# Where the rows of q and k stand: row 16 d + t instead of row 8 t + d

## The chip, the cores and the metric

The kernel runs on one core of one Trainium2 chip. Its time is the device time of one execution in microseconds (us). TensorE (PE in the profile) multiplies matrices, VectorE (DVE), ScalarE (ACT) and GpSimd (POOL) do the rest, and SyncE (SP) issues most of the transfers (DMAs). On-chip memory (SBUF) has 128 rows, called partitions.

## The reference, cut to what matters

The input x is 8 sequences of 256 tokens with 128 features. Three layers are added to it in turn:

```python
x = x + 0.5 * ffn(layernorm(x))      # router over 8 experts, top 2, hidden size 352
x = x + attention(layernorm(x))      # 16 heads of 8 dimensions
x = x + 0.5 * ffn(layernorm(x))
# in the attention, for each sequence b and head h:
q = q * cos + rotate_half(q) * sin;  k = k * cos + rotate_half(k) * sin
attn = q @ k.T * 8 ** -0.5 + alibi   # alibi: slope of the head * min(key - query, 0) * 8
w = softmax(attn);  out = w @ v
```

The change concerns only the product of q and k.

## The kernel before, in words

**Three phases.** `blocks(0)` is the first FFN: tokens are scattered by expert into 39 blocks of 128 rows, each block goes through the expert's matrices, and the results are scattered back. Then comes the attention with the second router, sequence by sequence. `blocks(1)` is the second FFN, built as the first one. The order of all instructions on every engine is written out by hand, and semaphores join the engines.

**q and k as sums of three bf16 parts.** After the rotation, q and k of one sequence are fp32. POOL and ACT cut them into three bf16 tiles that add up to the fp32 value: `lev[:, level, s, :]`, with level 0 (high), 1 and 2 (low), and s 0 for q and 1 for k (`split_qk`, lines 428 to 432, and `part`, line 649). In `lev` dimension d of head h stands in partition 16 d + h. The product q·k is formed from six products of parts, `PAIRS` = (0,0), (1,0), (2,0), (0,1), (1,1), (0,2) (level of q, level of k). They are added up by one matrix product over the partitions: in the tiles `qs` (q) and `ks` (k), pair t has eight rows, one for each dimension d, and each row holds all 16 heads × 256 tokens (8 KB).

**`stack(b)`** (lines 334 to 345) brings the parts of sequence b there: for each level, for q and k, one DMA on SP's queue for each pair that takes that level. These are 12 DMAs for a sequence, each of 64 KB: 128 runs of 512 bytes (one d and one h), read from 128 partitions of `lev` and written to 8 partitions of `qs` or `ks`, sixteen runs in each. The counts for a sequence are six DMAs of level 0, four of level 1 and two of level 2.

**The other rows.** Six rows of the same tiles carry the part of alibi that lies beyond 128 tokens (`far_in`, `far_rows`), the last two carry the negated row maximum of the scores (`max_rows`, lines 347 to 352, two DMAs of 8 KB), and the remaining rows are zero. There are three buffers (`RING`).

**Scores, twice.** `scores_1` (line 1139, 126 rows) makes the scores with queries on the partitions, so that DVE can find each query's maximum (`row_max`, line 923). `max_T` turns the maxima, ACT and DVE split them in two (lines 655 and 928), and `max_rows` puts them into the tile of q. `scores_2` (line 1160, 128 rows) then makes the scores with keys on the partitions, less the maximum, and ACT takes the exponential (line 662).

**Order.** In front of the loop, `stack(0)`, `stack(1)` and `max_rows(0)` stand on SP; PE does `scores_1` of sequence 0 and ACT the split of sequence 1 (line 649), which waits for all of `stack(0)`, since it overwrites `lev`. In iteration b of the loop each engine goes through steps 0 to 15: PE does `scores_2` of sequence b and `scores_1` of b + 1, and SP issues, in this order, `grow` (256 KB that `combine` needs), `stack(b + 2)` and `max_rows(b + 1)`. The first `scores_2` of the next iteration waits for `max_rows`. All these DMAs share one queue, so what stands in front of `max_rows` in it is served first.

Of the kernel before, what the change touches and what calls it, by code (L numbers as in the profile page):

```python
# [15 lines left out]
P = 128  # L16
TB = N // P
NT = B * TB
H, HD = 16, 8
# [21 lines left out]
YP_ROWS = SCRAP + P * ZR  # L41

PAIRS = [(0, 0), (1, 0), (2, 0), (0, 1), (1, 1), (0, 2)]
QK_ROWS = len(PAIRS) * HD

S2_ROWS = 128
S1_ROWS = S2_ROWS - 2
VW = 32
RING = 3
# [11 lines left out]
def macaron(nc, x, small_w, w1, v1, w2, ffn_bias, proj_b, slopes, ident, dist, dist_t, rope, expert_ids,  # L61
            far, ones_rows, out):
    ctx = ExitStack()
    with ctx:
        ctx.enter_context(nc.allow_low_precision(reason="exact splits"))

        def sb(name, shape, dt=F32):
            return ctx.enter_context(nc.sbuf_tensor(name, shape, dt))

        def sem(name):  # L70
            return ctx.enter_context(nc.semaphore(name))
# [22 lines left out]
        qs, ks = [qk_rows[:, i] for i in range(RING)], [qk_rows[:, RING + i] for i in range(RING)]  # L94
# [8 lines left out]
        lev = sb("lev", [P, 3, 2, N], BF16)  # L103
# [74 lines left out]
        d_far = nc.dram_tensor("d_far", (3, 2, H, N), BF16, kind="Internal").ap()  # L178
# [16 lines left out]
        far_out, rows_landed, bias_added, half_done = sem("far_out"), sem("rows_landed"), sem("bias_added"), sem("half_done")  # L195
# [54 lines left out]
        def _(sp):  # L250
# [23 lines left out]
            def blocks(r):  # L274
# [19 lines left out]
                for n in range(first, first + NB):  # L294
                    if n % GS == 0 and n + XB < first + NB:
                        rows += loaded(mybir.EngineType.SP, tab_r, (n + XB - first) // GS, BLOCK_ROWS - 1)
                    if n + XB < first + NB:
                        sp.wait_ge(xbT_full, n // GS + 1)
                        sp.wait_ge(dest_done, n // GS + 1)
                        load(n + XB)  # L300
                    if n == 6:
                        far_in()
                    if n == 30:
                        far_rows()
# [12 lines left out]
            def far_in():  # L317
                sp.wait_ge(wu_lo_done, 1)
                sp.dma_start(far_v, far).then_inc(far_landed, 16)
                sp.wait_ge(zero_done, 2 * RING)  # L320
                for i in range(RING):
                    sp.dma_start(qs[i][QK_ROWS:QK_ROWS + 3, :, :], ones_rows[0:3]).then_inc(rows_landed, 16)
                    sp.dma_start(ks[i][QK_ROWS + 3:QK_ROWS + 6, :, :], ones_rows[3:6]).then_inc(rows_landed, 16)
                    sp.dma_start(ks[i][S1_ROWS:S2_ROWS, :, :], ones_rows[6:8]).then_inc(rows_landed, 16)

            def far_rows():
                sp.wait_ge(far_step, 5)
                sp.dma_start(d_far.rearrange("l s h n -> h l s n"), far_l).then_inc(far_out, 16)
                sp.wait_ge(far_out, 16)
                for i in range(RING):  # L330
                    sp.dma_start(ks[i][QK_ROWS:QK_ROWS + 3, :, :], d_far[:, 0]).then_inc(rows_landed, 16)
                    sp.dma_start(qs[i][QK_ROWS + 3:QK_ROWS + 6, :, :], d_far[:, 1]).then_inc(rows_landed, 16)

            def stack(b):

                q, k = qs[b % RING], ks[b % RING]
                if b >= RING:
                    sp.wait_ge(s2_full, 16 * (b - RING + 1))
                for level, made in ((0, 2), (1, 4), (2, 5)):
                    sp.wait_ge(split_step, b * 5 + made)  # L340
                    for s, dst in ((0, q), (1, k)):
                        for t, pair in enumerate(PAIRS):
                            if pair[s] == level:
                                sp.dma_start(dst[t * HD:(t + 1) * HD, :, :], lev[:, level, s, :]  # L344
                                             ).then_inc(stack_landed[b % RING], 16)

            def max_rows(b):
# [3 lines left out]
                sp.wait_ge(ml_done, b + 1)  # L351
                sp.dma_start(q[S1_ROWS + 1:S2_ROWS, :, :], ml[:, 1, :]).then_inc(mrow_landed, 16)

            blocks(0)
            stack(0)
            stack(1)
            max_rows(0)
            for b in range(B):
                if b + 3 < B:
                    if b:  # L360
                        sp.wait_ge(comb[0], 4 * (b + 3))
                    sp.dma_start(grow, pairs(0, b + 3)).then_inc(g_landed, 16)
                if b + 2 < B:
                    stack(b + 2)
                if b + 1 < B:
                    max_rows(b + 1)
# [656 lines left out]
        def _(pe):  # L1023
# [127 lines left out]
            def scores_2(b, j):  # L1151
# [6 lines left out]
                for a in range(2):  # L1158
                    h = 2 * hp + a
                    nc.tensor.matmul(o[:, a * N:(a + 1) * N], ks[b % RING][0:S2_ROWS, h, kt * P:(kt + 1) * P],  # L1160
                                     qs[b % RING][0:S2_ROWS, h, :], start=(a == 0), stop=False)
                o = o[:, :].rearrange("p (h n) -> p h n", h=2)[:, :, kt * P:(kt + 1) * P]
# [155 lines left out]
```

## Time and profile before

| | us |
|---|---|
| median of 3 runs (lowest, highest) | 573.76 (571.87, 573.95) |
| profiled execution, its own time | 576.06 |
| its span, first to last instruction | 573.9 |
| PE busy | 399.3 |
| DVE busy | 301.4 |
| POOL busy | 250.3 |
| ACT busy | 214.5 |

The first FFN takes the span up to about 168 us, the attention up to about 442 us, and the rest is the second FFN. "Busy" counts the time in which an engine executes. The "granted clock" is the share of its full speed that TensorE was allowed in a stretch; it is 1.00 or 0.50. "DMA share" is the mean busy share of the core's 16 DMA engines in a stretch, GB/s what they moved. In a timeline, `[3.48 <-DMA ...]` at the end of a line says how long the engine was idle before it and what released it.

### The profile page before, as it was taken

What the parts mean: (1) busy time and instruction counts of PE and PEld (TensorE: products, weight loads), DVE (VectorE), ACT (ScalarE), POOL (GpSimd) and SP (SyncE); (2) the same over time, 40 slices, a digit from 0 to 9 for tenths busy, and PEclk for the clock granted to TensorE, in tenths of its full rate; (3) what the DMA queues carried; (4) which work ended last, traced back from release to release, by engine and by line L of the source; (5) the groups of instructions that cost most, each with busy time, mean ns of one, the idle gap of its engine ahead of it and who ended that gap; (6) DMA issues with size and microseconds to landing.
All of it is one profiled execution on the core that took longest, in us unless ns stands there. A gap on an engine that the chain in (4) does not pass through costs nothing.

```text
span 573.9 us, 9982 instructions
## 1 busy us (share of the span) xinstructions
PE 399.3 (70%) x3132; PEld 338.4 (59%) x3132; DVE 301.4 (53%) x909; ACT 214.5 (37%) x481; POOL 250.3 (44%) x358
## 2 busy tenths in 40 slices
PE   2500097999942378888878879798977119999970
PEld 2500087999941256575756657576754119999970
DVE  3960055598634175546465746465622406565545
ACT  5500043455411123535454444535465113444420
POOL 8677437388534310303434342423242422855440
PEclk9999999899985587989898989899999558999995
DMA  9921212122220550504133241413000021222217
GB/s 292 197 85 51 83 47 71 53 61 57 62 83 3 52 55 21 69 8 51 43 42 53 33 62 23 45 25 48 15 21 6 24 92 39 63 65 67 57 37 220
DMA packets 51030, 35.60 MB, mean 62 GB/s; under 512 B 5898, under 2 KB 48106, under 8 KB 50938
## 3 DMA queue, kind: packets, MB, share of 16 engines
q1 hardware_dynamic: 45940, 24.16, 22.7%
q0 software_dynamic: 4896, 10.54, 5.4%
q8 instruction: 27, 0.44, 0.4%
q10 hardware_dynamic: 144, 0.27, 0.2%
q14 instruction: 23, 0.19, 0.1%
HBM read 15.97 MB, written 12.55 MB: 50 GB/s over the span
## 4 chain that ended last, share of the span: by engine, by line
POOL 27%; PE 25%; issue 22%; DVE 10%; DMA 9%; ACT 4%; SPq 3%; POOLq 0%; DVEq 0%; ACTq 0%
POOL yp L408 12%; POOL xs L394 7%; PE bank L1139 5%; DMA qk_rows<-wd 5%; PE bank L1160 3%; PE bank L1175 3%; DVE nm L923 3%; PE bank L1142 2%; PE bank L1143 2%; DVE scr L915 2%; PE bank L1121 2%; POOL xres L458 1%; SPq L344 1%; PE bank L1163 1%; POOL rstd L383 1%
## 5 line engine op out<-in xcount | busy, mean ns | idle before, releaser
L923 DVE TENSOR_REDUCE nm<-bank 128x2 f32<-128x512 f32 x128 | 84.4, 686 | 68.6 <-PE bank L1143 67.4
L408 POOL DMA_INDIRECT yp<-scr,dest x78 | 76.4, 979 | 75.5 <-ACT scr L609 70.3
L662 ACT ACTIVATE stage<-bank 128x512 f32<-128x512 f32 x128 | 75.1, 596 | 85.0 <-PE bank L1164 83.9
L1063 PE MATMUL bank<-wu,xbT_hi 128*128 x156 | 65.7, 421 | 2.5 <-DVE xbT_lo L852 2.5
L1139 PE MATMUL bank<-qk_rows 126*128 126x256 bf16 x256 | 55.1, 300 | 17.0 <-DVE nm L923 9.6
L1078 PE MATMUL bank<-wd,scr 128*128 (+1 forms) x468 | 66.2, 278 | 0.3
L1078 PEld LDWEIGHTS bank<-wd,scr 128*128 128x128 f32 (+1 forms) x468 | 62.2, 194 | 0.6 <-issue 0.6
L1160 PE MATMUL bank<-qk_rows 128*128 128x256 bf16 x256 | 51.7, 285 | 11.6 <-DMA qk_rows<-wd 11.6
L859 DVE COPY scr<-bank 128x256 f32<-128x256 f32 x78 | 33.0, 424 | 49.7 <-PE bank L1072 49.3
L1054 PE MATMUL bank<-idn,scr 128*128 128x128 f32 x78 | 14.4, 297 | 62.7 <-DMA scr<-xs 62.7
L1065 PE MATMUL bank<-wu,xbT_hi 128*128 x156 | 52.5, 336 | 0.0
L1064 PE MATMUL bank<-wu,xbT_lo 128*128 x156 | 52.3, 335 | 0.0
L1142 PE MATMUL bank<-near_hi,idn_r 128*128 128x256 f32 x128 | 50.3, 393 | 0.0
L1054 PEld LDWEIGHTS bank<-idn,scr 128*128 128x128 f32 x78 | 10.7, 154 | 63.9 <-issue 63.3
L1163 PE MATMUL bank<-near_hi,idn_r 128*128 128x256 f32 x128 | 48.2, 377 | 0.0
L609 ACT ACTIVATE scr<-bank 128x128 f32<-128x128 f32 x78 | 21.7, 278 | 64.1 <-PE bank L1078 60.2
L873 DVE TENSOR_TENSOR scr<-bank,scr 128x352 f32<-128x352 f32 x78 | 40.8, 523 | 7.1 <-PE bank L1065 5.1
L428 POOL TENSOR_TENSOR scr<-scr 128x512 f32<-128x512 f32 x8 | 10.2, 1279 | 78.0 <-DVE scr L915 78.0
L852 DVE TENSOR_TENSOR xbT_lo<-bank,xbT_hi 128x384 fp32r<-128x384 f32 x26 | 14.4, 556 | 52.0 <-ACT xbT_hi L603 51.9
L619 ACT ACTIVATE scr<-bank 128x352 f32<-128x352 f32 x78 | 36.2, 464 | 13.2 <-PE bank L1065 13.2
L1072 PE MATMUL bank<-idn,scr 128*128 128x128 f32 (+1 forms) x234 | 39.7, 279 | 0.3 <-DVE scr L873 0.3
L603 ACT ACTIVATE xbT_hi<-bank 128x384 fp32r<-128x384 f32 x26 | 12.8, 490 | 70.6 <-PE bank L1054 70.6
(157 smaller groups left out, 901.8 us busy)
## 6 DMA issues: line engine op xcount, KB each, us to landing
qk_rows<-lev SPq DMA_DIRECT2D x96, 64.0 KB
scr<-xs SPq DMA_DIRECT2D x78, 64.5 KB
stage<-yp SPq DMA_DIRECT2D x11, 256.0 KB, 4.8
stage<-in_w SPq DMA_DIRECT2D x8, 176.0 KB, 3.9
stage<-in_v SPq DMA_DIRECT2D x8, 176.0 KB, 4.9
scr<-yp SPq DMA_DIRECT2D x5, 256.0 KB, 4.5
yp<-scr,dest POOLq DMA_INDIRECT x78
xres<-in_x SPq DMA_DIRECT2D x4, 256.0 KB, 5.0
```

The costliest lines, as they stand in the source:

```text
L408: nc.gpsimd.indirect_dma_start(out=yp[r][:, :], out_offset=bass.IndirectOffsetOnAxis(ap=dest[:, n:n + 1], axis=0), in_=ysb[:, n % YS, :], ...
L662: nc.scalar.activation(probs[:, g % RING, kt, 2 * (hp % 2):2 * (hp % 2) + 2, :], psS2[(b * 16 + j) % 3][:, :].rearrange("p (h n) -> p h n" ...
L873: nc.vector.tensor_tensor(hid[:, n % 2, :], up_v[n % 2][:, 0:F], gel[:, n % 2, :], ALU.mult).then_inc(hid_done, 1)
L923: nc.vector.tensor_reduce(nm[:, qt, 2 * hp:2 * hp + 2], psS1[i % 2][:, :].rearrange("p (h n) -> p h n", h=2), AX.X, ALU.max, negate=True). ...
L1063: nc.tensor.matmul(dst, hi, moving(n, a), start=True, stop=False)
L1064: nc.tensor.matmul(dst, lo, moving(n, a), start=False, stop=False)
L1065: nc.tensor.matmul(dst, hi, moving(n, a + 2 * F), start=False, stop=True).then_inc(done, 1)
L1078: i = nc.tensor.matmul(psH[n % 3][:, 3 * P:4 * P], hTs[0:w, n % 2, k * P:(k + 1) * P], wd[0:w, bass.ds(experts[n - first], 1), k, :].rearr ...
L1139: nc.tensor.matmul(o[:, j * N:(j + 1) * N], qs[b % RING][0:S1_ROWS, h, qt * P:(qt + 1) * P], ks[b % RING][0:S1_ROWS, h, :], start=(j == 0) ...
L1142: nc.tensor.matmul(o, idn_r[:, :], near_hi[0][:, 2 * hp:2 * hp + 2, :], start=False, stop=False)
L1160: nc.tensor.matmul(o[:, a * N:(a + 1) * N], ks[b % RING][0:S2_ROWS, h, kt * P:(kt + 1) * P], qs[b % RING][0:S2_ROWS, h, :], start=(a == 0) ...
L1163: nc.tensor.matmul(o, idn_r[:, :], near_hi[1][:, 2 * hp:2 * hp + 2, :], start=False, stop=False)
```

## The change

The eight rows of a pair no longer stand side by side. Dimension d of pair t goes to partition 16 d + t instead of 8 t + d, so each of the 12 DMAs writes to 8 partitions that stand 16 apart. The six alibi rows move from partitions 48 to 53 to 6 to 11, which pairs 0 to 5 leave free. Sizes and counts of all DMAs, and all operand shapes of TensorE, stay as they are.

```diff
 PAIRS = [(0, 0), (1, 0), (2, 0), (0, 1), (1, 1), (0, 2)]
-QK_ROWS = len(PAIRS) * HD
-S2_ROWS = 128
+SPREAD = P // HD
+FAR = len(PAIRS)
+S2_ROWS = P
@@ far_in
-                    sp.dma_start(qs[i][QK_ROWS:QK_ROWS + 3, :, :], ones_rows[0:3]).then_inc(rows_landed, 16)
-                    sp.dma_start(ks[i][QK_ROWS + 3:QK_ROWS + 6, :, :], ones_rows[3:6]).then_inc(rows_landed, 16)
+                    sp.dma_start(qs[i][FAR:FAR + 3, :, :], ones_rows[0:3]).then_inc(rows_landed, 16)
+                    sp.dma_start(ks[i][FAR + 3:FAR + 6, :, :], ones_rows[3:6]).then_inc(rows_landed, 16)
@@ far_rows
-                    sp.dma_start(ks[i][QK_ROWS:QK_ROWS + 3, :, :], d_far[:, 0]).then_inc(rows_landed, 16)
-                    sp.dma_start(qs[i][QK_ROWS + 3:QK_ROWS + 6, :, :], d_far[:, 1]).then_inc(rows_landed, 16)
+                    sp.dma_start(ks[i][FAR:FAR + 3, :, :], d_far[:, 0]).then_inc(rows_landed, 16)
+                    sp.dma_start(qs[i][FAR + 3:FAR + 6, :, :], d_far[:, 1]).then_inc(rows_landed, 16)
@@ stack
-                                sp.dma_start(dst[t * HD:(t + 1) * HD, :, :], lev[:, level, s, :]
+                                sp.dma_start(dst[t::SPREAD, :, :], lev[:, level, s, :]
                                              ).then_inc(stack_landed[b % RING], 16)
```

## Rows read from the trace of the kernel before

**Rows 1.** The page's chain that ended last, shares of the span by line.
```profile
POOL yp L408 12%; POOL xs L394 7%; PE bank L1139 5%; DMA qk_rows<-wd 5%; PE bank L1160 3%; PE bank L1175 3%; DVE nm L923 3%; PE bank L1142 2%; PE bank L1143 2%; DVE scr L915 2%; PE bank L1121 2%; POOL xres L458 1%; SPq L344 1%; PE bank L1163 1%; POOL rstd L383 1%
```
**Rows 2.** That chain in order of time: start us, duration us, what.
```profile
214.40 1.84 DMA qk_rows<-wd
...
240.60 5.07 DMA qk_rows<-wd
...
271.68 4.42 DMA qk_rows<-wd
...
364.01 4.83 DMA qk_rows<-wd
```
**Rows 3.** Timeline of PE at the first `scores_2` of sequences 1 to 6.
```profile
245.71 0.61 PE L1160 MATMUL bank<-qk_rows 128*128 128x256 bf16 x2 [3.48 <-DMA qk_rows<-wd]
...
276.14 0.55 PE L1160 MATMUL bank<-qk_rows 128*128 128x256 bf16 x2 [0.91 <-DMA qk_rows<-wd]
...
307.06 0.61 PE L1160 MATMUL bank<-qk_rows 128*128 128x256 bf16 x2 [1.36 <-DMA qk_rows<-wd]
...
338.09 0.61 PE L1160 MATMUL bank<-qk_rows 128*128 128x256 bf16 x2 [1.48 <-DMA qk_rows<-wd]
...
368.89 0.61 PE L1160 MATMUL bank<-qk_rows 128*128 128x256 bf16 x2 [1.40 <-DMA qk_rows<-wd]
...
398.05 0.38 PE L1160 MATMUL bank<-qk_rows 128*128 128x256 bf16 x2
```
**Rows 4.** Timeline of SP's queue: start us, us of issuing, line, transfers.
```profile
191.49 1.27 SPq L344 DMA_DIRECT2D qk_rows<-lev  x2
...
231.19 8.75 SPq L344 DMA_DIRECT2D qk_rows<-lev  x12
...
383.75 8.38 SPq L344 DMA_DIRECT2D qk_rows<-lev  x12
...
394.78 0.58 SPq L352 DMA_DIRECT2D qk_rows<-wd  x1
```
**Rows 5.** Stretches: window us, its length, granted clock, DMA share, GB/s.
```profile
186.00:187.00 1.00, 0.50 0.31 79
...
190.00:191.00 1.00, 0.50 0.65 61
...
198.00:199.00 1.00, 0.50 0.02 1
...
216.00:217.00 1.00, 0.50 0.42 123
...
393.00:394.00 1.00, 1.00 0.62 97
...
396.00:397.00 1.00, 1.00 0.04 9
```
**Rows 6.** Timeline in front of the loop: start us, us, engine, line.
```profile
184.74 23.56 SPq L344 DMA_DIRECT2D qk_rows<-lev  x24
...
193.18 1.41 DVE L915 TENSOR_TENSOR scr<-bank,rope_sb 64x512 f32<-64x512 f32 x2
194.73 1.26 POOL L428 TENSOR_TENSOR scr<-scr 128x512 f32<-128x512 f32 x1 [4.53 <-DVE scr L915]
...
199.82 0.63 ACT L649 ACTIVATE lev<-scr 128x512 bf16<-128x512 f32 x1 [9.52 <-DMA qk_rows<-lev]
199.82 0.58 PE L1139 MATMUL bank<-qk_rows 126*128 126x256 bf16 x2 [7.40 <-issue]
```
**Rows 7.** Stretches: window us, its length, PE busy, granted clock, DMA share, GB/s.
```profile
245.52:248.93 3.41, 3.22 (x15) 0.50 0.00 0
...
368.40:371.81 3.41, 2.92 (x14) 0.50 0.07 24
...
395.70:399.10 3.40, 3.02 (x33) 1.00 0.02 4
```
**Rows 8.** Waits: engine, line, waited for: us in total, times, longest us.
```profile
PE bank L1187 <- ACT scr L669: 14.3, 10, 1.8
```

## The prediction

> **What bounds the kernel now.** I read the chain of waits first, then who waited for whom, then the timelines of PE and SP around the places found, and last DMA share, GB/s and clock in short stretches.
>
> The chain by line [rows 1] shows two FFN phases that go by GpSimd's scatters (lines 408 and 394), which the change doesn't touch, and an attention phase in which PE's lines 1139, 1160 and 1175, DVE's line 923 and one transfer take turns. That transfer, 5% of the chain, is `max_rows` (qk_rows<-wd): 8 KB a time. In order of time [rows 2] it takes 1.84 us at its first place (sequence 0) and 4.4 to 5.1 us at the five places after it (three are shown). The bytes are the same each time. What differs is what stands in front of it in the queue: at the first place `stack(1)` had its last byte moved before; at the other five, the 12 transfers of `stack(b + 2)` were issued shortly before it. `stack(2)` was issued from 231.19 to 239.94 [rows 4], `max_rows(1)` at 240.60 [rows 2].
>
> PE pays for it at the first `scores_2` of a sequence [rows 3]: idle 3.48, 0.91, 1.36, 1.48 and 1.40 us before sequences 1 to 5, 8.63 us together. Sequence 6 has no such wait, so there something else ends last.
>
> How fast the stack moves is seen in front of the loop, where nothing else runs [rows 5]. The issue begins at 184.74 [rows 6] and the twelfth ends at 191.49 + 1.27 = 192.76 [rows 4], 0.67 us each. The data move at 79 GB/s in the first stretch, later at 61 GB/s with the DMA engines busier (share 0.65 against 0.31), and end just after 198. Then it isn't the issue that limits, it is the drain: 65.5 KB at 61 GB/s are 1.07 us a transfer, 12.9 us for twelve, against 8.0 us of issue. The time an engine spends on a 512-byte run follows from share and rate: 0.31 × 16 / 79 × 0.512 = 0.032 us in the first stretch, 0.65 × 16 / 61 × 0.512 = 0.087 us in the slow part. A transfer that writes to all 128 partitions (`grow`, at 216) runs at 123 GB/s with 0.42 × 16 / 123 × 0.512 = 0.028 us for a run of the same size. So the engines aren't starved in the slow part; each run is held up. What sets the stack apart is that all its 128 runs go into 8 neighbouring partitions.
>
> **The change, part by part.**
>
> *The destination of the 96 stack transfers.* The number of transfers, runs and bytes and the issue stay; only the destination is spread. If the hold-up is where neighbouring partitions are written, a run should cost something between 0.032 us and 0.087 us. The source is read in rows 16 d + h all along, also in the fast first stretch, so a pattern 16 apart has a row that speaks for it. To keep pace with an issue of 0.67 us, a transfer must fall from 1.07 us to 0.67, a factor of 1.6. At the cost of the fast row it would be 1.07 × 0.032 / 0.087 = 0.39 us. I take it that the drain keeps pace with the issue; the other ends are no gain (1.07 us stays) and a loss (below).
>
> *In front of the loop.* Now PE's first `scores_1` starts at 199.82 after 7.40 us idle, and ACT's split of sequence 1 at the same time after 9.52 us for the stack [rows 6]. With the drain at the issue's pace the twelfth transfer, issued at 192.76 − 0.64 = 192.12, lands 1.84 us [rows 2] to 2.4 later, at 194.0 to 194.5. What is late next is `rotate(1)` on DVE, which ends at 193.18 + 1.41 = 194.59 [rows 6] and stands in front of the row maxima on DVE and is waited for by PE. PE starts at 194.7: 5.1 us earlier. The split of sequence 1 also needs POOL's sum after the rotation, which ends at 194.73 + 1.26 = 195.99, so it starts 3.8 us earlier, at 196.0, and `stack(1)`, issued after its 0.63 us, begins at 196.7 and is done at 196.7 + 8.0 + 2 = 206.7. That is before `max_rows(0)`, which moves from 214.40 to 209.3. So all 5.1 us reach the first step of the loop. Bounds: 0 if the drain stays; 5.1 at most, because DVE holds it.
>
> *In the loop, the waits.* `max_rows` will find an empty queue. I give it 1.84 us as at its first place; the row of sequence 6 bounds it from above, where it was issued at 394.78 [rows 4] and PE went on at 398.05 [rows 3] without waiting, 3.27 us. Before sequence 1 PE is ready at 245.71 − 3.48 = 242.23 and the transfer lands at 240.60 + 1.84 = 242.44 to 243.87, in place of 245.67: 1.8 to 3.2 us, I take 3.0. Before sequence 2 PE is ready at 276.14 − 0.91 = 275.23, which is 3.55 us after the issue at 271.68; before sequence 5 it is 368.89 − 1.40 − 364.01 = 3.48 us. Both are more than 3.27, so the four waits go whole: 0.91 + 1.36 + 1.48 + 1.40 = 5.15 us. Sum of both: 8.15 us.
>
> Sequence 6 shows that the rest of an iteration can go on like this. `stack(7)` moved at 97 GB/s in its late part and was over by 397 [rows 5], and PE went from sequence 5 to 6 with no wait for a transfer [rows 3].
>
> *The clock.* After each of the five waits TensorE's clock stands at 0.50 (1.2 GHz) for 3.41 us; the first and the last of the five stretches are shown [rows 7]. PE is busy 3.22 and 2.92 us of them, and at 1.00 (2.4 GHz) the same work would take half, so one stretch costs 1.5 to 1.6 us, five 7.8. After sequence 6's beginning, with no idle time ahead of it, the clock stayed at 1.00 [rows 7]. But PE has other idle time in every iteration: ten waits of up to 1.8 us for ACT's line 669 [rows 8]. In this run none of them brought the clock down; when iterations get shorter, some may. I take three of the five stretches as won, 4.7 us; bounds 0 and 7.8.
>
> The Trainium skill's page "TensorE: Matmul & The Clock Gate" (section "Part 1: The HAM clock gate") says that idleness throttles the engine to half rate and activity releases it; the five stretches here, each next to an idle wait, agree, and neither page nor rows say which of the remaining waits will do it.
>
> *The alibi rows, the zero rows, PE.* The nine small transfers of `far_in` and six of `far_rows` run beside the first FFN and only change their address: 0. PE reads 126 or 128 partitions of the same tiles in the same shapes: 0. If one of these weren't hidden, it would be some tenths of a microsecond, once.
>
> **The sum.** 5.1 + 3.0 + 5.15 + 4.7 = 17.95 us. Against the profiled execution's own time, 576.06 (span 573.9 and 2.1 around it), that is 558.1. The median of the runs shown is 573.76, 2.3 lower; from it, 573.76 − 17.95 = 555.8. I predict 556.0 for the median. With no stretch of clock won it is 560.5, with all five 552.7.
>
> The Trainium skill's page "SBUF — State Buffer" (section "Door 1: The DMA port swizzle") speaks against a gain of eight: four neighbouring partitions share a port, a step of 32 stays on it and a step of 64 leaves it. By that, 8 t to 8 t + 7 reach two ports and 16 d + t four; at the page's 27.2 GB/s a port, two give 54 GB/s (61 measured here) and four 109 GB/s, an estimate of 0.60 us a transfer, just under the issue's 0.67. The sum would be the same, with little to spare.
>
> **The rivals.**
>
> *Half relief.* The spread helps, but the drain stays behind the issue, say at 0.85 us a transfer. For: 61 to 97 GB/s appear within the old layout already, so a transfer's rate isn't one fixed number; the new one may be another in between. Then twelve take 10.2 us in place of 12.9. In front of the loop 2.7 us come earlier; before sequence 1 2.7; the four others still vanish (all are below 2.7): 5.15; two stretches of clock, 3.1. Together 13.7: 560.1.
>
> *The destination isn't what limits.* The eight-fold shape may put a transfer on few engines, or reading `lev` may be slow, and both stay. For: the six transfers that read one tile at the same level share its partitions. Against: the same reads go at 0.032 us a run before the backlog builds up [rows 5], and an engine short of work would show less busy share, not double. Then nothing moves: 573.8. On the engines, the skill's page "DMA: Bandwidth & Descriptors" (section "Why a DMA increments its semaphore by 16 and not by 1") says that a transfer takes the largest number up to 16 that divides the outer sizes of both sides; with 8 and 128 that is 8 engines before and after. By that rule the change brings no engine, and if their number limited, this rival holds. No row here counts engines.
>
> *Slower: rows 16 apart collide.* If partitions 16 apart share one way in, the eight rows of a pair meet where now they were spread over at least two. At twice the cost a transfer takes 2.1 us, a stack 25.7. In front of the loop two stacks come behind each other: 2 × 12.9 = 25.8 us later. In the loop the stack issued at 231.19 would end at about 258, and `max_rows` behind it, 12 us later than now, for six sequences: 72 us. Together about 98: 672. It decides from about 1.1 us a transfer on; at 1.2 us it is 12 × 0.13 = 1.6 us at each of eight places, 587. Against it: the reading side does just this pattern at 0.032 us a run.
>
> **How the numbers follow.** The forecast 0.66, its own range 552 to 561. Half relief 0.15 (560). Destination not the limit 0.12 (573.8). Collision 0.05, of which most is below 590. The last 0.02 are more than forecast, if the loop's own balance gets better still. What a measurement of this kernel can tell from no change is about 0.5%, 2.9 us. Faster by more: 0.66 + 0.15 + 0.02 and a little of the third, 0.85. Within: 0.09. Slower: 0.06. Range 549 to 566: the forecast and half relief with their bounds; the third and fourth case are left out.
>
> **What would show each step.** In front of the loop: GB/s of the stack near 98 to its end (65.5 KB in 0.67 us), share of DMA below 0.5, and PE's first `scores_1` at 194.7, with DVE's line 915 as what it waited for. In the loop: the transfer of `max_rows` at 1.8 to 2.5 us in the chain at all places, PE's wait for it under 1 us before sequence 1 and none after. Clock: two stretches at 0.50 or fewer between the first sequence and the seventh, beside idle time that isn't a transfer's. I am wrong if the stack still moves at 61 GB/s, or if the waits go and the same time comes back as a wait of PE for ACT or DVE.

## The result, and the profile after

The changed kernel takes 555.46 us (median of 4 runs, 554.55 to 558.52), the kernel before in the same comparison 572.82 (4 runs, 569.78 to 573.95). The ratio is 0.9714 with an interval of 0.9658 to 0.977: faster by 2.9%, some 16 us. Forecast were 556.0 us and 17.95 us. The profiled execution took 556.09, its span is 554.3. The profiled execution of the kernel before (576.06) took longer than any of its four timed runs, so differences between the two traces can come out larger than that of the medians.

The stack first. These are stretches of the kernel after (window in us from the span's start, its length, granted clock, DMA share, GB/s), to be read against [rows 5]:

```profile
184.00:185.00 1.00, 0.50 0.38 92
...
188.00:189.00 1.00, 0.50 0.42 111
...
190.00:191.00 1.00, 0.50 0.42 112
...
192.00:193.00 1.00, 0.50 0.00 0
```

It moves at 92 to 112 GB/s nearly to its end, in place of 61, and the DMA engines are busy 0.4 of the time in place of 0.65. By 192.0 all is moved, a little over 9 us after the first issue (182.65); before it was just after 198, a little over 13 us after 184.74. PE's timeline and SP's queue (start us, duration us, line, in brackets the idle time before and what ended it):

```profile
182.65 19.59 SPq L346 DMA_DIRECT2D qk_rows<-lev  x24
...
192.56 0.61 PE L1141 MATMUL bank<-qk_rows 126*128 126x256 bf16 x2 [2.23 <-DVE scr L917]
...
208.91 0.61 PE L1162 MATMUL bank<-qk_rows 128*128 128x256 bf16 x2 [2.96 <-DMA qk_rows<-wd]
...
264.33 0.38 PE L1162 MATMUL bank<-qk_rows 128*128 128x256 bf16 x2
...
377.24 0.38 PE L1162 MATMUL bank<-qk_rows 128*128 128x256 bf16 x2
...
403.77 0.38 PE L1162 MATMUL bank<-qk_rows 128*128 128x256 bf16 x2
```

In front of the loop PE starts 9.91 us after the first issue, before it was 15.08 [rows 6], and what ends its wait is DVE's rotation, not a transfer. In the loop the rows without brackets tell the rest (sequences 2, 6 and 7 are shown): at the first `scores_2` of sequences 1 to 7 PE no longer waits for anything [rows 3]. The second transfer of `max_rows` lands like this (us from issue to landing, over the eight sequences), in the kernel before and now:

```profile
DMA to landing us min/median/max: 1.8/4.6/5.1
...
DMA to landing us min/median/max: 1.8/1.8/2.8
```

The clock (window, length, PE busy, granted clock, DMA share, GB/s), and what PE still waits for (us in total, times, longest us):

```profile
223.68:227.09 3.41, 3.41 (x23) 0.50 0.27 70
315.84:319.25 3.41, 3.41 (x27) 0.50 0.13 39
...
397.76:401.17 3.41, 3.41 (x22) 0.50 0.04 10
```
```profile
PE bank L1189 <- ACT scr L671: 14.4, 10, 1.9
```

Five stretches at half clock between the `scores_2` of sequence 0 and those of sequence 7 have become three, at other places. Each of the three begins within 1.6 us after the end of an idle stretch of 1.8 us: the first of a wait for DVE's row maximum (PE idle up to 222.10), the other two of waits for ACT's line 671 (up to 315.23 and 397.44). Those waits are as they were [rows 8]; of the six waits of 1.79 to 1.85 us for line 671 in this loop, two have such a stretch beside them and four have none.

What the clock gave back shows in PE's busy time, as PE's work is the same. The loop from the first `scores_2` of sequence 0 to the scatter of the last sequence but one, in the kernel before, in the changed kernel, and in a second trace of it (the run `again` below); window, length, PE busy (records), clock, DMA share, GB/s:

```profile
216.30:442.60 226.30, 191.50 (x1711) 0.95 0.25 35
...
208.90:423.30 214.40, 188.05 (x1711) 0.97 0.14 37
...
212.90:429.40 216.50, 188.35 (x1711) 0.97 0.13 37
```

PE is busy 3.45 and 3.15 us less for as many records.

Where the profiled span got shorter, from one to the next (before, after, change of the part, in us):

| part | before | after | change |
|---|---|---|---|
| up to the first issue of the stack (first FFN, start of the attention) | 184.74 | 182.65 | −2.09 |
| first issue to PE's first `scores_1` | 15.08 | 9.91 | −5.17 |
| from there to the first `scores_2` of sequence 0 | 16.47 | 16.35 | −0.12 |
| loop, to the scatter of the last sequence but one (at 442.57 and 423.35) | 226.28 | 214.44 | −11.84 |
| the rest | 131.33 | 130.95 | −0.38 |

The first line isn't the change's work, as far as can be told. That phase is the same in both kernels but for the address of the alibi rows, and its end fell between 182.20 and 186.66 us in the nine traces of the whole kernel. In the second trace of the changed kernel the loop took 216.43 us, 9.85 less than before in place of 11.84.

### The profile page after: what moved, and what is told of

Its sections match the earlier page's. It is cut to its first block, busy times and chain, and to the rows that moved or that the text cites. A ratio compares the mean times of both kernels' runs of the same rounds, so it can differ in the third digit from the quotient of the medians.

```text
span 554.3 us, 9982 instructions
## 1 busy us (share of the span) xinstructions
PE 392.9 (71%) x3132; PEld 331.7 (60%) x3132; DVE 300.7 (54%) x909; ACT 214.5 (39%) x481; POOL 250.7 (45%) x358
## 4 chain that ended last, share of the span: by engine, by line
PE 29%; POOL 28%; issue 21%; DVE 12%; DMA 5%; ACT 3%; SPq 1%; POOLq 0%; ACTq 0%; DVEq 0%
POOL yp L410 13%; POOL xs L396 7%; PE bank L1141 5%; PE bank L1177 5%; PE bank L1162 4%; DVE nm L925 3%; PE bank L1144 2%; PE bank L1145 2%; DVE scr L917 2%; PE bank L1165 2%; PE bank L1166 2%; PE bank L1123 2%; POOL rstd L385 2%; POOL xres L460 2%; DMA stage<-yp 1%
## 5 line engine op out<-in xcount | busy, mean ns | idle before, releaser
L1065 PE MATMUL bank<-wu,xbT_hi 128*128 x156 | 64.9, 416 | 2.5 <-DVE xbT_lo L854 2.5
L1141 PE MATMUL bank<-qk_rows 126*128 126x256 bf16 x256 | 52.3, 287 | 11.9 <-DVE nm L925 9.7
L1067 PE MATMUL bank<-wu,xbT_hi 128*128 x156 | 52.1, 334 | 0.0
L1165 PE MATMUL bank<-near_hi,idn_r 128*128 128x256 f32 x128 | 48.2, 377 | 0.0
L1144 PE MATMUL bank<-near_hi,idn_r 128*128 128x256 f32 x128 | 48.1, 376 | 0.0
L396 POOL DMA_INDIRECT xs<-qk_rows,pos x32 | 32.1, 1004 | 12.1 <-issue 9.4
```

Of the source, the lines that this page charges most:

```text
L396: nc.gpsimd.indirect_dma_start(out=xs[r][:, :], out_offset=bass.IndirectOffsetOnAxis(ap=pos[:, k, t:t + 1], axis=0), in_=src(t, k), in_off ...
L1065: nc.tensor.matmul(dst, hi, moving(n, a), start=True, stop=False)
L1067: nc.tensor.matmul(dst, hi, moving(n, a + 2 * F), start=False, stop=True).then_inc(done, 1)
L1141: nc.tensor.matmul(o[:, j * N:(j + 1) * N], qs[b % RING][0:S1_ROWS, h, qt * P:(qt + 1) * P], ks[b % RING][0:S1_ROWS, h, :], start=(j == 0) ...
L1144: nc.tensor.matmul(o, idn_r[:, :], near_hi[0][:, 2 * hp:2 * hp + 2, :], start=False, stop=False)
L1165: nc.tensor.matmul(o, idn_r[:, :], near_hi[1][:, 2 * hp:2 * hp + 2, :], start=False, stop=False)
```

## The experiments

Each edit is against the changed kernel, unless it says before. Times of one group were taken on one chip and go by their ratio to the kernel before on it; "on the basis of 572.82" is that ratio times 572.82 us. Lines left out are marked `...` or named.

**Which rows limit a transfer.** Two runs with nothing but transfers, one after the other.

```diff
+CASES = [(8, 1), (8, 16), (8, 8), (8, 2), (8, 4), (16, 1), (16, 8), (32, 1), (32, 4), (4, 1), (4, 32), (4, 4), (8, 1), (8, 16)]
...
+            for i, (rows, step) in enumerate(CASES):
+                to = dst[0:(rows - 1) * step + 1:step, 0:512 // rows * N].rearrange("d (c n) -> d c n", n=N)
+                of = src[:, :, 0:N]
+                sp.dma_start(to, of).then_inc(landed[i], 16)
+                sp.wait_ge(landed[i], 16)
```

> Only 14 transfers, one after the other, each of 512 runs of 512 bytes from 128 partitions of one tile to R rows of another, S apart; the layer itself is left out and the output is zero. Theory (what limits is the way into the destination rows; each way in takes about 61 / 2 = 31 GB/s): 8 rows side by side 61 GB/s; 8 rows 16, 8 or 2 apart about 122; 8 rows 4 apart about 150 (8 engines at 0.028 us a run); 16 rows side by side 122; 16 rows 8 apart and 32 rows side by side about 245; 32 rows 4 apart more; 4 rows side by side 31; 4 rows 32 apart 61; 4 rows 4 apart 75. Rival (the number of engines on a transfer limits, and goes with the number of rows): 8 rows take the same at every step, 16 rows twice the rate of 8, 4 rows half. Rival (any two neighbouring rows disturb each other, without fixed groups): 4 rows 32 apart as fast as 4 rows 4 apart.

Each line is one transfer, from its first byte to its last within 0.1 us, in the order of the list up to (4, 4): window, length, clock, DMA share, GB/s. (The two cases that end the list repeat the first two, at 60 and 97 GB/s.)

```profile
6.50:10.90 4.40, 1.00 0.54 60
14.10:16.80 2.70, 1.00 0.46 95
19.10:21.90 2.80, 1.00 0.45 94
24.40:27.00 2.60, 1.00 0.45 101
29.00:31.50 2.50, 1.00 0.44 105
33.20:35.00 1.80, 1.00 0.84 142
37.90:39.30 1.40, 1.00 0.78 183
41.20:42.80 1.60, 1.00 1.00 164
45.70:46.80 1.10, 1.00 0.80 238
48.30:57.90 9.60, 1.00 0.28 27
60.80:66.20 5.40, 1.00 0.22 48
67.90:72.70 4.80, 1.00 0.22 55
```

Eight neighbouring rows take 60 GB/s, the rate of the old stack alone and without any other work. The same eight rows 2, 4, 8 or 16 apart take 94 to 105. So the destination does it, and the rival by which the number of rows alone counts falls: same rows, same runs, 1.6 times the rate. But my figures of 122 and 150 for the spread cases were too high, and so was 245 for sixteen rows 8 apart (183) and for 32 side by side (164). Eight rows don't pass 105 however they lie, four don't pass 55, sixteen side by side reach 142: beside the place of the rows there is a pace that goes with their number, some 13 GB/s for each up to eight rows. In the changed kernel this second limit lies at the pace of the issue (65.5 KB in 0.64 us are 102 GB/s), and no run separates the two. The rival of neighbours without fixed groups isn't decided by four rows 32 apart against 4 apart (48 and 55); the second list decides it.

> Again only transfers of 512 runs of 512 bytes one after the other (the layer is left out, the output is zero), now all wide enough for 16 engines: R rows, S apart. Theory (rows fall into fixed groups of eight, each with one way in of about 27 GB/s; a group is four neighbours and the four 32 further on, so 16 rows side by side reach 4 groups, 16 rows 2, 4 or 8 apart 8, 32 rows 1 or 2 apart and 64 rows side by side 8, 32 rows 4 apart, 64 rows 2 apart and all 128 rows 16): 32 rows 2 apart are no faster than 32 side by side (near 150 GB/s), 64 side by side no faster than 32, and 32 rows 4 apart, 64 rows 2 apart and 128 rows are the fast ones (250 or more). Rival (a group is eight neighbouring rows): 32 rows 2 apart twice as fast as 32 side by side, 64 side by side too.

The second list: (16, 1), (16, 2), (16, 4), (32, 1), (32, 2), (32, 4), (64, 1), (64, 2) and (128, 1).

```profile
6.50:8.40 1.90, 1.00 0.83 138
11.30:12.60 1.30, 1.00 0.83 197
14.40:15.80 1.40, 1.00 0.79 187
21.00:22.60 1.60, 1.00 0.96 164
25.40:26.80 1.40, 1.00 0.97 187
29.40:30.40 1.00, 1.00 0.87 260
32.00:33.40 1.40, 1.00 1.01 185
36.10:37.10 1.00, 1.00 0.91 256
38.70:39.70 1.00, 1.00 0.93 262
```

This speaks for the groups. 64 rows side by side (185) are little faster than 32 (164), and 32 rows 2 apart (187) as fast as 64: all three reach eight groups by the rule of four neighbours and the four 32 further on. 32 rows 4 apart reach sixteen, and run at 260, as fast as all 128. The rival, groups of eight neighbours, had 64 side by side and 32 two apart at twice the rate of 32 side by side; 1.1 times came out. The rival of any two neighbours falls too: no row of the 32 two apart has a direct neighbour, and they are no faster than 64 side by side. What isn't borne out is a fixed pace of 27 GB/s for each group: two groups take 60 (8 rows side by side), four 138 to 142 (16 side by side), eight 164 to 197, sixteen 238 to 262, with windows read to 0.1 us. The page "SBUF — State Buffer" of the Trainium skill (section "Door 1: The DMA port swizzle") gives this map, and the runs agree with it. Its table has 218 GB/s as what eight groups tend to, and 189 and 196 as measured for 1 MiB; the 164 to 197 here are for 262 KB.

**Another spread.**

```diff
-SPREAD = P // HD
-FAR = len(PAIRS)
+FIRST = [0, 1, 2, 3, 32, 33]
+FAR = 64
...
-                                sp.dma_start(dst[t::SPREAD, :, :], lev[:, level, s, :]
+                                sp.dma_start(dst[FIRST[t]:FIRST[t] + 29:4, :, :], lev[:, level, s, :]
```

> The changed kernel with the eight rows of a pair 4 apart instead of 16 (pairs 0 to 3 in rows 0 to 31, pairs 4 and 5 in 32 to 63, alibi rows 64 to 69). Theory: the issue of 0.64 us a transfer is what is left, so nothing moves: 555.5, within 0.5% of the changed kernel, the stack at 100 GB/s. Rival (16 apart is special, because the reading side goes 16 apart too): the stack falls back toward 61 GB/s and the time toward 573.

560.7 us, ratio 0.9738 (0.9672 to 0.9804), against 0.9714 (0.9658 to 0.977) for 16 apart: no difference can be seen. The stack went at 98 GB/s. Sixteen apart isn't special, and a layout that reaches eight groups in place of four brings nothing that can be seen. The issue (102 GB/s) and the pace of eight rows (94 to 105) would explain that.

**Half of the pairs spread.**

```diff
-FAR = len(PAIRS)
+NEAR = {3: 3, 4: 19, 5: 35}
+FAR = 51
...
-                                sp.dma_start(dst[t::SPREAD, :, :], lev[:, level, s, :]
+                                sp.dma_start(dst[t::SPREAD, :, :] if t < 3 else dst[NEAR[t]:NEAR[t] + HD, :, :], lev[:, level, s, :]
```

> The changed kernel with pairs 0 to 2 in rows 16 d + t and pairs 3 to 5 in eight neighbouring rows each (3 to 10, 19 to 26, 35 to 42), so 6 of the 12 transfers of a stack are as before. Theory: these six take 1.07 us against 0.64 of issue, so a stack drains up to 2 us later than with all spread and 2 to 3 us earlier than before. In front of the loop PE starts 0 to 2 us later than in the changed kernel, in the loop max_rows lands before PE is ready except for sequence 1 (under 1.5 us): 556 to 559. Rival (neighbouring rows of any transfer hold up the whole queue): nearer to 565 than to 556.

561.56 us on that chip, ratio 0.9772 (0.9697 to 0.9848); on the basis of 572.82 that is 559.8, just beyond my 559. In the trace PE starts 195.68 − 184.41 = 11.27 us after the first issue, between 9.91 and 15.08 and nearer to the first. It waits 0.42 us before sequence 1 and not at all before the others:

```profile
195.68 0.58 PE L1142 MATMUL bank<-qk_rows 126*128 126x256 bf16 x2 [3.59 <-issue]
...
238.61 0.39 PE L1163 MATMUL bank<-qk_rows 128*128 128x256 bf16 x2 [0.42 <-DMA qk_rows<-wd]
```

Half of the spread brings most of the gain; my reading is that each wait, but the first, needed only 0.9 to 1.5 us. The times alone can't tell this kernel from the changed one.

**The old rows in one buffer of three**, which sequences 2 and 5 use. (`far_in` and `far_rows` take `FAR[i]` for `FAR`, left out here.)

```diff
-FAR = len(PAIRS)
+FAR = [6, 6, 48]
...
-                                sp.dma_start(dst[t::SPREAD, :, :], lev[:, level, s, :]
+                                sp.dma_start(dst[t * HD:(t + 1) * HD, :, :] if b % RING == 2 else dst[t::SPREAD, :, :], lev[:, level, s, :]
```

> The changed kernel with the old rows in one of the three buffers, the one that sequences 2 and 5 use. Theory: only the stacks of 2 and 5 are slow, so PE waits for max_rows before sequence 1 (about 3.5 us) and before sequence 4 (about 1.5 us) and nowhere else in the loop, the clock is at half for 3.4 us after each of the two (1.6 us each), and the start in front of the loop stays as in the changed kernel (sequences 0 and 1 have the new rows): 555.5 + 5.0 + up to 3.2 = 560 to 564. Rival (the gain comes from something common to all sequences, such as the product over other rows): no wait appears at 1 and 4.

564.92 us there, ratio 0.9832 (0.9762 to 0.9901), or 563.2 on the basis of 572.82. All waits of PE for `max_rows` in this kernel; the first is that of sequence 0, which every trace has:

```profile
208.49 0.61 PE L1162 MATMUL bank<-qk_rows 128*128 128x256 bf16 x2 [2.97 <-DMA qk_rows<-wd]
...
238.28 0.61 PE L1162 MATMUL bank<-qk_rows 128*128 128x256 bf16 x2 [4.02 <-DMA qk_rows<-wd]
...
327.13 0.39 PE L1162 MATMUL bank<-qk_rows 128*128 128x256 bf16 x2 [0.90 <-DMA qk_rows<-wd]
```

The two others stand before sequences 1 and 4, behind the slow stacks of 2 and 5, and nowhere else, as forecast; they are 4.02 and 0.90 us, forecast were 3.5 and 1.5. At the first the clock was at half for 6.8 us (237.37 to 244.20), twice what was forecast, at the second it didn't fall. This is the run that ties the waits to the rows of the stack, one by one.

**`max_rows` on a queue of its own**, with the old rows. Edit against the kernel before (SP's own `max_rows`, taken out, isn't shown):

```diff
-            max_rows(0)
...
-                if b + 1 < B:
-                    max_rows(b + 1)
...
+            def max_rows(b):
+                q = qs[b % RING]
+                act.wait_ge(ml_hi, b + 1)
+                act.dma_start(q[S1_ROWS:S1_ROWS + 1, :, :], ml[:, 0, :]).then_inc(mrow_landed, 16)
+                act.wait_ge(ml_done, b + 1)
+                act.dma_start(q[S1_ROWS + 1:S2_ROWS, :, :], ml[:, 1, :]).then_inc(mrow_landed, 16)
...
             max_high(0)
+            max_rows(0)
...
                         max_high(b + 1)
+                        max_rows(b + 1)
```

> The kernel before, rows as they were, with the two transfers of max_rows issued on ScalarE's queue instead of SP's. Theory (max_rows is late only because it stands behind the stack in one queue): on its own queue it lands in about 2 to 3 us, PE's waits before sequences 1 to 5 go, though the stack moves at 61 GB/s as before; in front of the loop the 5 us stay lost. That is 8.6 us of waits and up to 3 of clock less, some tenths a sequence more on ACT for the issue: ratio 0.980 to 0.988. Rival (the engines are held up by the stack's runs whatever the queue): max_rows still takes over 4 us and the time stays within 0.5% of before.

578.86 us against 575.23, ratio 1.0057 (1.0013 to 1.0101): not faster, if anything slower. My theory of this run was too simple. The second transfer now lands as in the first line here, and PE still waits before sequences 1, 3 and 4 (the first is shown, after the landing times, us min, median and max):

```profile
DMA to landing us min/median/max: 1.9/3.7/5.5
...
246.32 0.39 PE L1159 MATMUL bank<-qk_rows 128*128 128x256 bf16 x2 [2.59 <-DMA qk_rows<-wd]
```

The waits sum to 2.59 + 1.65 + 0.69 = 4.9 us in place of 8.6. So a queue of its own takes away less than half of the waits: with the stack in flight the 8 KB are late from another queue too. That the same DMA engines serve both queues fits this; no run here shows it. The rival was nearer. In the profiled execution the stretch from the first issue to the scatter of the last sequence but one was 4.3 us shorter than in the trace of the kernel before, and the timed runs show none of it. The profiled execution is the fastest of this kernel's ten (575.58 of 575.58 to 581.35), so that trace flatters it. Whether something else took the gain back (ACT now issues, and waits for DVE before it does) isn't known.

**ACT's order turned round at step 10**, for the claim on the clock, and as a version that might beat both.

```diff
+                    if s == 10 and b < B:
+                        oT_copy(b, 0)
                     if s == 10 and b >= 1:
                         if b >= 3:
                             act.wait_ge(scat2[(b - 1) % 2], 64 * ((b - 1) // 2))
                         ln_apply(2, b - 1, 2 * b - 2, TB, lambda t: xn2[:, (t // TB) % 2, t % TB, 0:D])
-                    if s == 10 and b < B:
-                        oT_copy(b, 0)
```

> The changed kernel with ACT's order at step 10 turned round: the copy of the attention's output (line 671 there) ahead of the second normalization's two activations, which wait for GpSimd. Theory (that wait of 1.8 us is PE's longest idle stretch in an iteration now, and what brings the clock down in the changed kernel): it falls to about 0.6 us and 0.3 before the next transpose, 0.9 us for each of seven sequences, and the two or three stretches at half clock go, 1.6 us each: 6 to 11 us less than the changed kernel, 545 to 552. Rival (DVE sets the pace of the iteration, PE's idle time only moves): within 2 us of the changed kernel. Rival for the clock: the stretches come back elsewhere.

> The changed kernel once more, for a direct comparison with the others of this group and for a second trace. Theory: the ratio of 0.971 to the kernel before comes again; in front of the loop PE starts 9.9 us after the first issue of the stack (15.1 before), no wait for max_rows before sequences 1 to 6, and the clock falls at most three times between sequence 0 and the second FFN, next to waits for ACT's line 671, at places that may differ from the first trace.

The changed kernel again: 560.63 us, ratio 0.9708 (0.9647 to 0.977), the same as in its first comparison. PE starts 196.17 − 186.26 = 9.91 us after the first issue, no wait for `max_rows` before sequences 1 to 7. The clock fell three times after sequence 0 had started (226.04, 376.22 and 403.53), the first next to the wait of 1.78 us for DVE's row maximum, which the forecast didn't have, the others next to a wait for line 671.

With ACT's order turned: 553.37 us, ratio 0.9598 (0.9543 to 0.9653), 1.1% below the changed kernel's ratio, 7.3 us by the medians, and 549.8 on the basis of 572.82, inside the forecast. The six runs (549.83 to 554.67) all lie below the six of the changed kernel (556.16 to 564.25), so the rival by which PE's idle time only moves falls. The wait is down to 0.55 us on average, and from 214.60 us on the loop ran at full clock (waits; then window, length, PE busy, clock, DMA share, GB/s):

```profile
PE bank L1189 <- ACT scr L671: 5.5, 10, 0.7
```
```profile
214.60:422.70 208.10, 182.88 (x1698) 1.00 0.14 39
```

The wait for line 671 shrank as forecast. On the clock the theory fits for line 671: no stretch at half clock stands next to it in this trace or the next. The wait for DVE's row maximum in sequence 0 (1.78 us) is still there; in the next run a stretch at half clock begins 1.4 us after it (225.69), in this one none does, so the same wait has such a stretch in one execution and not in another. The other traces say the same: between sequences 0 and 7 there is one such stretch with half of the pairs spread, two with the rows 4 apart, three in each trace of the changed kernel, all with the waits for line 671 untouched. One trace a kernel is thin evidence for a count of stretches. **PE's transpose one step later on top of it:**

```diff
-                    if s == 11 and b >= 1:
+                    if s == 12 and b >= 1:
                         if b + 2 < B:
                             pe.wait_ge(sin_done, 2 * b + 6)
```

> As the run before, and PE's transpose for the second router (ln_T of the second FFN) one step later, behind the scores of step 12, so that PE need not wait for the normalization just moved back. Theory: the remaining 0.3 us a sequence goes too, 1 to 3 us less than with ACT's order alone. Rival: the router's chain (logits, ranks, positions) starts later and its wait takes the place of it, as much or more.

551.95 us, ratio 0.9568 (0.9514 to 0.9622): the best median of all, 4.3% below the kernel before, but its interval and its runs overlap with those of the run before it. That it gains over it isn't shown.

## Why the prediction was right, point by point

**The destination limits the stack.** Right, and shown by itself: 60 GB/s into eight neighbouring rows, 94 to 105 into spread ones.

**In front of the loop.** Forecast 5.1 us, with DVE's rotation as what is late next. Measured 9.91 us from the first issue in both traces of the changed kernel, so 5.17 less than before, with that releaser.

**The waits in the loop.** Forecast 3.0 + 5.15 = 8.15 us; all 8.63 went. Before sequence 1 I had left half a microsecond; in that iteration the clock fell once (223.68), PE was later by itself, and the transfer no longer mattered. With ACT's order turned, where the clock didn't fall there, PE waited 0.20 us for the transfer before sequence 1. `max_rows` lands in 1.8 us in the median, as assumed, and in 2.8 at its longest. The run with one old buffer brought the waits back where it should.

**The clock.** Forecast that three of the five stretches go, 4.7 us; in number two went, and the sign "two stretches at 0.50 or fewer" didn't come true. The loop as a whole is 11.84 us shorter, less 8.63 of waits that leaves 3.2 us, about two stretches at 1.6. PE's busy time says the same: 3.45 us less, 3.15 in the second trace. This is the one term that was sized too high, by some 1.5 us. In the second trace the loop is only 9.85 us shorter, which leaves 1.2; there PE waited 0.9 us more for DVE's row maximum, and the rest is open. That other idle time would go with a fall of the clock was named as the risk, and stretches at half clock stand next to waits for line 671 twice in each trace of the changed kernel; with these waits cut down, none did. One reading of mine was off without harm: the stretches of [rows 7] don't begin after the waits but 0.19 and 0.49 us before PE goes on, at 245.71 and 368.89.

**The sum.** Forecast 17.95; measured 17.36 by the medians and 16.4 by the ratio. In the profiled executions it is 19.97, of which 2.09 come from ahead of the stack. The forecast's four terms give 5.17 + 8.63 + 3.2 = 17.0 in the first trace, and 5.17 + 9.85 = 15.0 in the second; the interval of the ratio is 13 to 20 us. That the forecast of 556.0 meets the median within 0.5 us is closer than the runs can tell, and in part luck: a clock term too high by 1.5 stands against waits that were 0.5 too low and a starting median 0.9 above that of the comparison.

**The rivals.** Half relief: doesn't hold, the new rate is near 98 GB/s. But it is held by the issue or by a pace of about 13 GB/s a row, which lie at the same place, so this rival was closer to coming true than I thought. Destination not the limit: falls. Its argument on the number of engines was half right, since eight rows do have a ceiling of 105 GB/s, only it lies above 61. Collision of rows 16 apart: falls, 95 GB/s.

## What to carry to other kernels

A small transfer that is late although its queue has little to do may stand behind a large one whose destination lies in a few neighbouring partitions; look at GB/s and at the DMA share together. Here 61 GB/s at a share of 0.65 was a hold-up at the destination, and with the rows spread it was 98 GB/s at 0.37. Spreading the rows costs nothing where a product sums over partitions, as any order of them will do. A gap closed on TensorE may pay twice, since here every stretch at half clock in the loop stood next to a gap of 0.9 us or more; how many go isn't foreseen by counting gaps, since others of 1.8 us remain.

## What the runs showed of the hardware that I had not expected

The pace by the number of destination rows: up to 55 GB/s for four rows, 105 for eight, 183 to 197 for sixteen in eight groups, and no more than 262 for 32, 64 or 128 rows in all sixteen groups. The page "DMA: Bandwidth & Descriptors" of the Trainium skill (section "Why a DMA increments its semaphore by 16 and not by 1") has a transfer run on the largest number of engines, up to 16, that divides the outer sizes of both sides; the rates go with it, in steps of about 13 GB/s a row up to eight and with an end near 260. The DMA share goes the same way, 0.22 to 0.28 for four rows, 0.44 to 0.54 for eight and 0.78 to 1.01 from sixteen on; no run counts the engines themselves. For eight rows the two limits are 60 GB/s side by side and 94 to 105 spread.

A second queue protects a small transfer only in part from a congested large one: 3.7 us in the median to landing, against 4.6 behind it in the same queue and 1.8 with the congestion gone.

The stretch up to the first issue of the stack, the same work each time, took 182.2 to 186.7 us in nine traces. In the five longest (184.7 and more) the clock had been at half for 6.8 us around 100 us, in the four shortest not at all or for 3.4.
